# An indexer that stacks 32-query head products in one bank, 28 blocks picked by 0/1 products, and an earlier selection of tiles 1 to 5

## The reference, cut to what matters

```python
q_i = (x @ idx_wq).reshape(B_, L_, N_IDX_HEAD, D_HEAD)      # 4 index heads of 64
k_i = x @ idx_wk
s_i = jax.nn.relu(jnp.einsum('bthd,bsd->bths', q_i, k_i))
I = jnp.einsum('bths,h->bts', s_i, idx_w)                   # weighted sum over the 4 heads
I = jnp.where(local[None], jnp.inf, I)                      # the 64 newest keys always
I = jnp.where(causal[None], -jnp.inf, I)
_, idx = jax.lax.top_k(I, kk)                               # kk = 96
```

## Time and profile before

| | |
|---|---|
| median of 3 runs | 834.49 us (827.72 to 836.64) |
| the profiled execution | 826.53 us |
| its span, first to last instruction | 824.6 us |
| mean granted TensorE clock | 0.982 of full speed |
| busy PE / DVE / ACT / POOL | 770.4 / 648.0 / 508.7 / 507.6 us |

### The profile page before, as it was taken

How to read it: one execution, slowest core, us unless ns; L and a number is a source line. 1 busy time by engine, 2 the same in 40 slices (tenths; PEclk the granted TensorE clock), 3 DMA queues, 4 the chain that set the end, 5 groups by cost and what they waited for, 6 DMA issues and landing times.

```text
span 824.6 us, 17320 instructions
## 1 busy us (share of the span) xinstructions
PE 770.4 (93%) x5725; PEld 460.6 (56%) x5725; DVE 648.0 (79%) x1906; ACT 508.7 (62%) x1461; POOL 507.6 (62%) x530
## 2 busy tenths in 40 slices
PE   8787899999999999999999999999999988999986
PEld 4334456565656565656566566566668444545543
DVE  4879798888999998979899999942232679696863
ACT  5556586675877878788787886686623334344230
POOL 6777777777777777777777777777710733211210
PEclk9898899999999999999999999999999999999999
DMA  8412211212111111111111111139136100000000
GB/s 275 93 26 54 53 36 42 50 36 41 31 28 31 25 32 30 26 31 30 27 31 27 30 29 27 31 87 227 49 116 179 52 0 1 1 13 2 13 6 22
DMA packets 58825, 39.97 MB, mean 48 GB/s; under 512 B 26961, under 2 KB 49713, under 8 KB 58545
## 3 DMA queue, kind: packets, MB, share of 16 engines
q1 hardware_dynamic: 41568, 21.57, 10.2%
q0 software_dynamic: 14336, 15.72, 9.5%
q10 hardware_dynamic: 2832, 1.58, 0.7%
HBM read 33.31 MB, written 5.55 MB: 47 GB/s over the span
## 4 chain that ended last, share of the span: by engine, by line
PE 58%; DVE 16%; ACT 9%; issue 8%; POOL 5%; DMA 2%; POOLq 0%; DVEq 0%; ACTq 0%; SPq 0%
PE psI L663 7%; PE psK L647 5%; ACT R L928 4%; PE psP L828 3%; PE psK L766 3%; PE psS L1771 3%; PE psS L802 3%; PE psP L835 3%; PE psK L754 3%; PE psP L817 2%; PE psS L805 2%; PE psP L647 2%; DVE SC L1144 2%; POOL R L1554 2%; PE psS L845 2%
## 5 line engine op out<-in xcount | busy, mean ns | idle before, releaser
L630 POOL DMA_INDIRECT G<-key_rows,idx x320 | 322.0, 1006 | 100.5 <-issue 95.2
L663 PE MATMUL psI<-kiT,qiT 64*128 64x512 f32 (+5 forms) x320 | 85.7, 559 | 13.6 <-ACT R L928 12.3
L647 PE MATMUL psK<-cst 128*128 128x512 bf16 x339 | 93.6, 383 | 1.3 <-ACT KT L1034 1.3
L1058 ACT ACTIVATE PT<-psP 128x256 f32<-128x256 f32 x128 | 48.4, 378 | 69.9 <-PE psP L835 64.5
L1144 DVE SCALAR_TENSOR_TENSOR SC<-R,w_x,SC 128x512 f32<-128x512 f32 (+5 forms) x120 | 78.5, 654 | 11.6 <-ACT R L928 8.5
L1172 DVE MAX8 top<-SC 128x8 f32<-128x128 f32 (+15 forms) x64 | 78.4, 1225 | 2.4
L1174 DVE FIND_INDEX8 idxf<-top,SC 128x8 uint32<-128x128 f32 (+15 forms) x64 | 78.3, 1223 | 0.0
L928 ACT ACTIVATE R<-psI 128x512 f32<-128x512 f32 (+5 forms) x160 | 73.3, 510 | 6.3 <-PE psI L663 4.8
L1562 POOL TENSOR_SCALAR rstd<-mv 128x4 f32<-128x4 f32 x13 | 3.6, 275 | 116.1 <-DVE mv L1978 116.1
L1026 ACT ACTIVATE PR<-PR,rinv 128x208 f32<-128x208 f32 x128 | 58.5, 457 | 26.2 <-DVE rinv L1335 25.6
L1034 ACT ACTIVATE KT<-psK 96x512 f32<-96x512 f32 x108 | 63.8, 591 | 15.6 <-PE psK L754 14.7
(11 more groups left out here) (352 smaller groups left out, 1725.0 us busy)
## 6 DMA issues: line engine op xcount, KB each, us to landing
G<-key_rows,idx POOLq DMA_INDIRECT x320, 2.5
rtmp<-idx_rows SPq DMA_DIRECT2D x20, 128.0 KB, 3.2
xslots<-zrow SPq DMA_DIRECT2D x4, 320.0 KB, 11.2
SC<-xslots SPq DMA_DIRECT2D x8, 160.0 KB, 2.5
yslots<-SC ACTq DMA_DIRECT2D x8, 160.0 KB, 2.4
V<-val_rows SPq DMA_DIRECT2D x15, 80.0 KB
xr<-in_x SPq DMA_DIRECT2D x1, 1024.0 KB, 11.7
qiT<-in_w_gate SPq DMA_DIRECT2D x4, 256.0 KB, 4.0
```

The source lines that it names most:

```text
L630: pool.indirect_dma_start(ring[o % RING][:, g % GPB, DR:], None, key_rows, bass.IndirectOffsetOnAxis(ap=idx[:, t, g:g + 1], axis=0),).then ...
L647: pe.matmul(ps[:, :].rearrange("p (a n) -> p a n", a=2), warm_w, warm_x, start=True, stop=True, skip_group_check=True)
L663: pe.matmul(psI[i][:, 0:w], lhs, kiT[64 * i:64 * i + 64, CH * c:CH * c + w], start=True, stop=True).then_inc(s["i_mm"], 1)
```

## The change

**Heads stacked.** A pair step now handles 64 queries with all four heads instead of 128 queries with two heads: in each of psI0 and psI1, four products of 64 rows by 32 queries go to the four 32-partition strips. Head h reads rows 0-63 or 64-127 by its parity, and in the second bank its strip is swapped with its neighbour's (h ^ 1). So one pair is 8 products (64x32) where it was 2 (64x128). After relu, the partition of R is (head, query in 32).

**Sum on PE.** `head_sum` multiplies R by a [128, 32] matrix of the head weights (four products of 128 rows by 32 columns into the four strips of psX), which gives the weighted sum for 128 queries. ACT copies it into SC (`sum_copy`). DVE's `combine` and ACT's L935 are gone; the mask is added just before the first top operation.

**Blocks.** `HOT` gains blocks 12 to 15 and 20 to 23 (2 and 3 matrices each, 20 in all): 96 blocks are gathered instead of 104, and the first gathered one is block 28 instead of 12. Before the products of a hot block PE now runs 2 fillers (`WARM_H`), before those of a gathered block 1 instead of 2 (10 stays), and the one before `p_transpose` has 384 columns instead of 512.

**Router.** psX belongs to the head sums, so the router uses the last 128 columns of psP. ACT copies logits and counts (`logits_copy`, `counts_copy`). PE waits for the `o_copy` of the running step before the three router products and before the next `p_transpose` for the copy of what they wrote, and they stand ahead of `scores` in the step.

**Plan.** Before step 0 the room is 2.2 a step; tiles 1 to 5 have a level of 3.2 of their own, the others one that is searched from 1.0 (it comes to 3.06). By it tile 1 is selected by step -13, tile 2 by -11, tile 3 by -8, tile 4 by -4, tile 5 by 0, tile 6 by 7, tile 7 by 19, tile 8 by 31, tile 9 by 43 and tile 15 by 113. Three operations of tile 6 stand in step 1.

```diff
-HOT = (4, 5, 6, 7, 8, 9, 10, 11, 16, 17, 18, 19, 24, 25, 26, 27, 32, 33, 34, 35)
+HOT = (4, 5, 6, 7, 8, 9, 10, 11, 12, 13, 14, 15, 16, 17, 18, 19, 20, 21, 22, 23, 24, 25, 26, 27, 32, 33, 34, 35)
-WARM_FIRST, WARM_GAP, WARM_TILE, WARM_K, WARM_P, WARM_T = 9, 2, 10, 2, 1, 0
+WARM_FIRST, WARM_GAP, WARM_TILE, WARM_K, WARM_P, WARM_T, WARM_H = 9, 2, 10, 1, 1, 0, 2
-START_ROOM = 1.1
+START_ROOM, LEAD, LEAD_LEVEL, SPREAD = 2.2, 5, 3.2, (4, 9)
@@ index_pair
                     for i in range(2):
-                        lhs = qiT[64 * i:64 * i + 64, pair, P * t:P * (t + 1)]
-                        pe.matmul(psI[i][:, 0:w], lhs, kiT[64 * i:64 * i + 64, CH * c:CH * c + w],
-                                  start=True, stop=True).then_inc(s["i_mm"], 1)
+                        for h in range(NIH):
+                            rows, at = slice(64 * (h % 2), 64 * (h % 2) + 64), QPG * (h ^ i)
+                            lhs = qiT[rows, h // 2, P * t + QPG * (2 * pair + i):P * t + QPG * (2 * pair + i + 1)]
+                            mm = pe.matmul(psI[i][at:at + QPG, 0:w], lhs, kiT[rows, CH * c:CH * c + w],
+                                           start=True, stop=True, skip_group_check=True)
+                        mm.then_inc(s["i_mm"], 1)
+                def head_sum(t, c):
...
+                    pe.wait_ge(s["i_relu"], 4 * (m + 1))
+                    for g in range(P // QPG):
+                        mm = pe.matmul(psX[QPG * g:QPG * (g + 1), 0:w], w_sum[:, g % 2, :], R[:, m % 2, g, 0:w],
+                                       start=True, stop=True, skip_group_check=True)
+                    mm.then_inc(s["comb"], 1)
@@ front_one_hot
+                    keep_warm(psK, WARM_H)
@@ p_transpose
+                    beside_free(n + LAG_T)
...
-                        keep_warm(psP, WARM_P if n + LAG_T < NT * NB else WARM_T)
+                        keep_warm_beside(WARM_P if n + LAG_T < NT * NB else WARM_T)
@@ scalar
+                def sum_copy(t, c):
...
+                    act.wait_ge(s["comb"], chunk_base(t) + c + 1)
+                    if c == 0 and t >= 2:
+                        act.wait_ge(s["topk"], TOP_STEPS * (t - 1))
+                    act.activation(SC[:, t % 2, CH * c:CH * c + w], psX[:, 0:w], ACT.Copy).then_inc(s["i_first"], 1)
@@ vector
-                    for h in range(1, NIH):
...
-                        dve.scalar_tensor_tensor(out=dst, in0=R[:, m % 2, h, 0:w], scalar=w_i[:, h:h + 1], in1=dst,
-                                                 op0=ALU.mult, op1=ALU.add).then_inc(s["comb"], 1)
```

More of the change, by code:

```diff
@@ L113, in key_tiles @@
     return -(-(P * t + QB * (b + 1) - LW) // P)
+KTM = max(key_tiles(m) for m in HOT)
 def hot_tiles(n):
@@ L139, with budget, cost @@
 INDEX_END = NB * (NT - 2) - -1
-START_ROOM = 1.1
+START_ROOM, LEAD, LEAD_LEVEL, SPREAD = 2.2, 5, 3.2, (4, 9)
+OTHER = (0.0, 0.9, 1.9, 1.3, 0.0, 0.6, 0.0, 0.8)
 TOP_STEPS = 12
 def index_plan():
[L149 to L160, removed]
+    def budget(n, level):
+        if n < 0:
+            return START_ROOM
+        return max(0.0, level - (0.7 if n >= 3 else 0.0) - OTHER[n % NB] - (0.25 * key_tiles(n) + 0.2 if n in HOT else 0.0))
+    def cost(t, i):
@@ L161, in cost @@
         return (1.04 * keys_of(t) / 1000 + 0.07) if i < TOP_STEPS - 1 else 0.1
-    other = (0.0, 0.9, 1.9, 1.3, 0.0, 0.6, 0.0, 0.8)
-    def hot(n):
-        return 0.25 * key_tiles(n) + 0.2 if n in HOT else 0.0
     def lay(level):
[L169 to L190, removed]
+        plan, done_at, top_end, n, left = {}, {m: N0 for m in range(chunk_base(3))}, {}, N0 + 1, 0.0
@@ new lines, in lay @@
+        for t in range(1, NT):
+            if t + 1 < NT and t + 1 >= 3:
+                for c in range(chunks_of(t + 1)):
+                    m = chunk_base(t + 1) + c
+                    at = n + (c + 1) * SPREAD[t > LEAD] // (chunks_of(t + 1) + 1)
+                    done_at[m] = max(at, done_at[m - 1] + 2, N0 + 4, top_end.get(t - 1, N0) + 2 if c == 0 else N0)
+            for k in range(TOP_STEPS):
+                ready = done_at[chunk_base(t + 1) - 1]
+                while left <= 0 or n < ready:
+                    n += 1
+                    left = min(left, 0.0) + budget(n, LEAD_LEVEL if t <= LEAD else level)
+                plan.setdefault(n, []).append((t, k))
+                left -= cost(t, k)
+            top_end[t] = n
@@ L196, in index_plan @@
     plan, done_at, _ = lay(level)
-    pairs = {}
+    pairs, sums = {}, {}
     for t in range(3, NT):
         for c in range(chunks_of(t)):
[L201 to L209, removed]
+            at = done_at[chunk_base(t) + c]
+            sums[at] = (t, c)
+            for u in range(2):
+                pairs[at - 4 + u] = (t, 2 * c + u)
+    return pairs, sums, plan
 C_ID = 0
@@ L648, in keep_warm, with keep_warm_beside @@
                                   skip_group_check=True)
+                def keep_warm_beside(count):
+                    for _ in range(count):
+                        pe.matmul(psP[:, 0:3 * P].rearrange("p (a n) -> p a n", a=2), warm_w, warm_beside, start=True,
+                                  stop=True, skip_group_check=True)
                 def index_pair(t, u):
@@ L946, in _ @@
                 act.preload_act_table_set("natural_log_exp_and_others")
+                act.wait_ge(s["ld_w"], 16)
+                for i in range(2):
+                    act.activation(w_sum[:, i, :], w_rows, ACT.Copy, scale=w_i[:, i:i + 1]).then_inc(s["w_cp"], 1)
                 def projected(c, parts):
@@ L1102, in _ @@
                         rank_copy()
-                    for t, u in index_pairs.get(n - 1, ()):
-                        relu_pair(t, u)
+                    if n in index_sums:
+                        sum_copy(*index_sums[n])
+                    if n - 1 in index_pairs:
+                        relu_pair(*index_pairs[n - 1])
                     if 0 <= n < NT * NB:
                         k_copy(n)
+                    if n in TILE_AT["x1_t"]:
+                        x1_copy(TILE_AT["x1_t"][n])
+                    if n in TILE_AT["router"] and TILE_AT["router"][n] < NT - 1:
+                        logits_copy(TILE_AT["router"][n])
+                    if n in TILE_AT["cumulate"] and TILE_AT["cumulate"][n] < NT - 1:
+                        counts_copy(TILE_AT["cumulate"][n])
                     if n == -NB:
@@ L2231 @@
             spread[3 * E1, col] = 1.0
+    idx_weights = np.stack([np.repeat(a("L0_attn_idx_w").reshape(NIH)[[h ^ i for h in range(NIH)]], QPG)
+                            for i in range(2)], 1)
     arrays = {
```

136 lines of the change are left out of this document (81 added, 55 removed).

## The result

| | before | after |
|---|---|---|
| median of the runs | 834.7 us (827.7 to 836.6) | **874.5 us** (872.4 to 879.3) |
| ratio | 1 | 1.0524, 95% interval 1.0474 to 1.0573 |
| the profiled execution, its span | 826.5, 824.6 us | 872.4, 870.5 us |
| mean granted clock | 0.982 | 0.979 |

A forecast was written before the change was run, and what follows sets the result against it. The prediction took PE's list, fillers included, as the bound, with POOL's gathers close behind. Its terms 17+10-6 = +21 us, added to the median of 834.5, gave 855.5 us, range 828 to 872.

The forecast's parts named there:

- rivals 1 and 3: Rival 1 (0.15): DVE is the bound, freeing it gives 818 us; rival 3 (0.07): small products take turns, 905 us.
- step 2 to 43: From the first score minimum (61.8 us before) to that of block 41 (239.85 us); forecast net +10 us.
- the group of head sums: Sign of a right forecast: the head sums take 30 to 35 us of PE.
- Fillers: 74 x 0.226 + 78 x 0.057 = -21: Step 43 to the attention's end: fewer and narrower fillers shorten PE's list by 21 us.
- should take half of PE's idle time: -4: Step 43 to the attention's end: DVE, freed of the sums, removes half of PE's 8.6 us idle time, -4 us.
- I forecast -6: Net change from step 43 to the end of the attention, 346 us before: -6 us.
- Net +17: Up to the first score minimum: earlier selections on DVE delay the first block by 17 us, bounds +8 to +22.
- I give back all 15: Steps 2 to 43: PE's 9.3 us idle and 5.9 us of lower clock pay 15 of its 25 us growth.
- Rival 2: Chance 0.24: the late start is made up as steps 2 to 14 run at PE's pace; about +5, 839.5 us.
- The pair's extra: Each pair in steps 2 to 43 costs about 0.08 us more after a change of shape, bounds 0 to 0.14.
- the rule that I set beside it: Trainium skill, Tiling Modes: a changed tiling mode drains the array, so pairs and head sums pay twice, perhaps +5 us.
- The limit that I set for the kernel after: POOL's gathers from step 43: 335 us plus some 5 to the last score minimum make 340, against 346.

The follow-up runs named there:

- a_sum2: The kernel after with the four products of every head sum issued twice: 895.4 us, ratio 1.0758 to the kernel before.
- a_k2: The kernel after with 2 fillers instead of 1 before a gathered block (90 more): 879.4 us, ratio 1.0597.
- n_k1: The kernel after with the 20 old hot blocks, the slow early pace and no fillers before hot blocks; 1 filler before gathered blocks: 847.6 us, 1.0231.
- b_fill: The kernel before with only the change's filler counts, 1 instead of 2 before gathered blocks and 2 before hot ones: 833.9 us, 1.0005.
- a_hot20: The kernel after with the 20 hot blocks of before (blocks 12 to 15 and 20 to 23 gathered again): 857.9 us, 1.0315.
- b_lead: The kernel before with a room of 2.2 instead of 1.1 a step before step 0: 832.2 us, 0.999.
- a_plan: The kernel after with selection paced as before (room 1.1, no own level for tiles 1 to 5): 869.6 us, 1.0459.
- u_bf16: The kernel after with old hot blocks, early pace and fillers restored, and R and the sum's weights in bf16: 837.9 us, 1.0066.
- a_noh: The kernel after without the two fillers before a hot block's 0/1 products (56 fillers): 862.8 us, 1.0364.
- n_k0: As n_k1, but no filler before a gathered block and 2 instead of 10 at each tile's third block: 848.9 us, 1.024.
- b_k0: The kernel before with no filler before a gathered block and 2 instead of 10 at each tile's third block: 834.9 us, 1.0032.

## Why the prediction was wrong

**What held.** The direction, and rivals 1 and 3 fall: DVE's waits for PE grew, the sums cost their full length between blocks 41 and 104 (a_sum2), and eight 64x32 products do run side by side (16 passes of 512 columns in 1.02 us). The growth of PE's busy time from step 2 to 43, forecast at 25 us, is 190.9-167.0 = 23.9. POOL's early idle time and the price of a head sum (0.9 forecast for 455 keys, 1.00 measured for 512) were right in kind. Of the signs, the transpose of tile 3's indices (47.3 us), the length of a pair and the last gather (616.2) came as said; the first minimum (84.1), block 41 (278.2) and the group of head sums (37.3 us) came above their ranges.

**Where it failed: "Fillers: 74 x 0.226 + 78 x 0.057 = -21".** I let each filler off PE's list return its full 0.226 us, because the chain of the middle was PE without a gap. From step 43 to the end 75 of them return 8.1 us of 17 in the kernel after (a_k2), and 8.2 with three parts undone (n_k1); in the kernel before 56 return 5.3 of 12.7 in the middle and nothing in the time (b_fill). Most of the rest turns into PE's waits for ACT's relu and copies, which a chain read through a full PE doesn't show. So the -21 was worth some 8. The same holds for "should take half of PE's idle time: -4": idle PE between the minima of blocks 41 and 104 grew from 6.3 to 11.3 us. These two terms are some 17 us too low. From step 43 to the end the time rose by 2 us where I forecast -6, and not by more because the late steps had less to select (see "Net +17" below).

**"I give back all 15".** I read PE's idle time and clock in a fixed stretch of time, 61.8 to 120 us, but the first 22 us of it lie ahead of the first block in the kernel after. By steps, from the first minimum to block 41, PE's idle time fell from 11.1 to 3.3 us, so 7.9 came back, and the mean granted clock is 0.96 in both kernels, so its 5.9 us did not. 23.9-7.9 = 16: steps 2 to 43 cost 16 us, not 10. The eight new hot blocks were underpriced: 8 us, or 11.6 with their fillers, against 17 by a_hot20; in the kernel before they cost 6. Why they cost more here is not shown.

**"Net +17 for the first block".** The start moved by 22 us, at the upper bound, but I was wrong to carry it to the end one for one. b_lead moves the start by 12 us for no cost, a_plan takes 12 away for 5. The steps behind have less to select, and PE's pairs and sums done early are not done later: with the late plan blocks 41 to 127 take 354.4 us (a_plan), with the early one 348.1. Rival 2 was right that a late start is partly made up, though behind block 41 and not in steps 2 to 14. That the forecast of 21 us came near half the loss is in part luck: the start carried in full, 12 us or more too much, covered the terms above.

**The pair's extra.** The pair of 1.13 us in the earlier trace rows began after a wait of 0.26 us, not after a change of shape, so it didn't price such a change, and didn't bear out the rule that I set beside it. A pair behind other shapes took 1.02 us in the kernel after.

**POOL.** The 335 us from block 64's first gather (281.2) to the last one (616.2) are as forecast by number only: 11 us of them are waits of POOL for the indices of the last tiles, and the last minimum comes 10 us behind the last gather, where it was 8 before. The limit that I set for the kernel after holds the kernel before more closely.

**The account by the runs**, in us: stacked heads, sums and router 25 (of these 20 for the sums' length by u_bf16, about 3 for the router), eight more hot blocks with their fillers 17, fillers before the other hot blocks 9 (40 of the 56 of a_noh), plan 5, 90 fillers fewer -6. That is 50 against 44 by the ratio, so the parts don't add up exactly; each is a difference of two ratios and carries 6 to 9 us of uncertainty, so the plan's 5 and the last -6 are not clear of noise. The first one, u_bf16's 20 and the 17 are.

**The chances.** 0.61 for slower was on the right side. The range failed at its upper end: it left no room for a saving in my own sum that doesn't come, while it reached down to two rivals.

## What to carry to other kernels

When a chain runs through one full engine, a second is 93% busy and a third works without a pause, work taken off the first buys a part of its length at best: here two fifths to a half of it behind block 41, and nothing in the time of the kernel before. Real work put onto the full engine cost its full length in the middle. Price additions and savings on the fullest engine differently: a removed filler is worth nothing until a run shows what stands behind it. Look for every list that is nearly full, also that of the engine which only issues gathers. Where a start is late because work was done ahead, look at what the later steps no longer have to do before you carry the delay to the end, and compare stretches by steps, not by the clock on the wall.

## What was not expected of the hardware

Eight products of 64 rows by 32 columns, f32, four of them in each of two banks, took 1.02 us for 512 columns, against 1.01 for the two 64x128 products that they replace, though I had put a change of shape at 0.08 us.

With the fillers before gathered blocks gone (those before `p_transpose` stayed, and 2 at each tile's third block), the granted clock of the middle differed between the two kernels: n_k0, 7% of PE idle, had 0.98 from 240 to 540 us and fell only behind 540 us, to 0.65 in the last seven blocks; the kernel before (b_k0), 10% idle, had 0.92 from 240 to 540 us.
